# Filling TensorE's wait before the end of every leaf with products that nobody reads

## What is computed

```python
def _L0_attn_ref(x, Wq, bq, Wk, bk, Wv, bv, Wo, bo):
    ...
    def step(carry, qkv):
        A, M = carry
        q, k, v = qkv
        s_t = jnp.sum(k * q, axis=-1, keepdims=True)
        u = k / (jnp.linalg.norm(k, axis=-1, keepdims=True) + EPS)
        Au = jnp.einsum('bij,bj->bi', A, u)
        denom = 1.0 + jnp.sum(u * Au, axis=-1, keepdims=True)
        A = A - jnp.einsum('bi,bj->bij', Au, Au) / denom[..., None]
        z = Au / denom
        alpha = s_t * z
        M = M + jnp.einsum('bi,bj->bij', v, alpha)
        o = jnp.einsum('bij,bj->bi', M, q)
        return ((A, M), o)
...
x = x + 0.5 * _L0_ffn_ref(_layernorm(x, axis=-1), L0_ffn_W1, L0_ffn_b1, L0_ffn_W2, L0_ffn_b2)
x = x + _L0_attn_ref(_layernorm(x, axis=-1), L0_attn_Wq, L0_attn_bq, L0_attn_Wk, L0_attn_bk, L0_attn_Wv, L0_attn_bv, L0_attn_Wo, L0_attn_bo)
x = x + 0.5 * _L0_ffn_ref(_layernorm(x, axis=-1), L0_ffn_W1, L0_ffn_b1, L0_ffn_W2, L0_ffn_b2)
```

## Time and profile before

| | us |
|---|---|
| median of 3 timed runs | 1063.75 |
| lowest and highest | 1062.14, 1065.49 |
| profiled execution | 1061.38 |
| its span, first to last instruction | 1059.7 |

### The profile page before, as it was taken

The page is one execution under the profiler, slowest core; times in us unless marked ns, Lnnn a source line. Parts: engine busy times, 40 slices in busy tenths (PEclk is TensorE's granted clock), DMA queues, the critical chain, the costliest instruction groups (busy, mean ns, idle before and its releaser), DMA issues.

```text
span 1059.7 us, 28459 instructions
## 1 busy us (share of the span) xinstructions
PE 921.2 (87%) x11675; PEld 710.7 (67%) x11675; DVE 786.7 (74%) x2504; ACT 544.5 (51%) x1096; POOL 304.7 (29%) x256
## 2 busy tenths in 40 slices
PE   4899999999998687588898838747799999999998
PEld 1477777777786666476796636546577777777766
DVE  6878788878679998887597979792666665665663
ACT  5678788878745344122344311101565665565574
POOL 4354445444311000000000000003756455455340
PEclk9899999999999898689899859786999999999999
DMA  5353639465437462144500000465524334234231
GB/s 161 70 140 87 166 98 213 127 138 131 121 119 213 146 158 61 41 123 120 161 21 2 5 4 4 135 135 135 130 61 114 86 92 116 73 101 100 40 80 60
DMA packets 170886, 108.28 MB, mean 102 GB/s; under 512 B 79360, under 2 KB 163712, under 8 KB 170112
## 3 DMA queue, kind: packets, MB, share of 16 engines
q1 hardware_dynamic: 153856, 89.62, 33.5%
q10 hardware_dynamic: 16896, 16.78, 5.2%
HBM read 44.96 MB, written 37.75 MB: 78 GB/s over the span
## 4 chain that ended last, share of the span: by engine, by line
PE 31%; DVE 15%; issue 2%; POOL 1%; DMA 1%; ACT 0%; SPq 0%; DVEq 0%; POOLq 0%
PE ldl_work L2043 10%; PE ldl_work L2031 10%; DVE lane_rows L1171 6%; DVE ldl_rank_one L1168 4%; PE ldl_work L2015 2%; DVE ldl_lane_dinv L1153 2%; PE ldl_work L1625 1%; PE ldl_work L2006 1%; PE ldl_work L1999 1%; PE ldl_work L1998 1%; DVE lane_rows L1149 1%; PE ldl_work L1985 1%; DVE lane_rows L1147 1%; PE ldl_work L1360 1%; PE ldl_work L1443 1%
## 5 line engine op out<-in xcount | busy, mean ns | idle before, releaser
L1796 POOL TENSOR_TENSOR T<-T,out_bv_rows 128x512 f32<-128x512 f32 x16 | 20.3, 1271 | 399.4 <-DVE out_s_over_d L1899 393.1
L446 DVE TENSOR_TENSOR ffn_h_rest<-ffn_ps_h,ffn_h_high 128x512 f16<-128x512 f32 x128 | 86.3, 685 | 53.7 <-ACT ffn_ps_h L631 53.2
L630 ACT ACTIVATE ffn_h_high<-ffn_ps_h,b_columns 128x512 f16<-128x512 f32 x128 | 87.9, 686 | 62.5 <-PE ffn_ps_h L712 62.0
L2043 PE MATMUL ldl_work<-w_ternary,ldl_panels 128*128 128x256 f16 x512 | 118.2, 273 | 0.0
L726 PE MATMUL ffn_ps_y<-w_ternary,ffn_h_high 128*128 128x256 f16 x512 | 117.8, 273 | 0.0
L726 PE MATMUL ffn_ps_y<-w_ternary,ffn_h_rest 128*128 128x256 f16 x512 | 117.8, 273 | 0.0
L712 PE MATMUL ffn_ps_h<-ffn_xT_high,w_ternary 128*128 128x512 f16 x256 | 98.6, 385 | 8.5 <-DVE ffn_h_rest L446 8.3
L712 PE MATMUL ffn_ps_h<-ffn_xT_rest,w_ternary 128*128 128x512 f16 x256 | 98.5, 385 | 0.0
L2031 PE MATMUL ldl_work<-out_xT_high,w_ternary 128*128 128x512 f16 x256 | 97.0, 379 | 0.0
L2031 PE MATMUL ldl_work<-out_xT_rest,w_ternary 128*128 128x512 f16 x256 | 97.0, 379 | 0.0
L1944 ACT ACTIVATE ldl_work<-ldl_work,b_columns 128x512 f32<-128x512 f32 x128 | 84.2, 658 | 0.0
(11 more groups left out here) (214 smaller groups left out, 2287.5 us busy)
## 6 DMA issues: line engine op xcount, KB each, us to landing
ffn_x<-in_x SPq DMA_DIRECT2D x16, 512.0 KB, 4.4
x_scratch<-ffn_x_out ACTq DMA_DIRECT2D x16, 512.0 KB, 3.3
aT_scratch<-ffn_aT SPq DMA_DIRECT2D x16, 512.0 KB, 5.1
inv_aT<-aT_scratch SPq DMA_DIRECT2D x16, 512.0 KB, 5.1
T<-x_scratch SPq DMA_DIRECT2D x16, 512.0 KB, 3.8
uT_scratch<-ffn_uT SPq DMA_DIRECT2D x16, 256.0 KB, 5.2
inv_uT<-uT_scratch SPq DMA_DIRECT2D x16, 256.0 KB, 4.1
qT_scratch<-inv_qT SPq DMA_DIRECT2D x16, 256.0 KB, 4.1
```

Of the source, the lines that this page charges most:

```text
L446: nc.vector.tensor_tensor(hl[n % 2][:, f], ps_h[f % 3][:], hh[n % 2][:, f], ALU.subtract).then_inc(hl_done, 1)
L630: nc.scalar.activation(hh[n % 2][:, f], ps_h[f % 3][:], ACT.Gelu, bias=c.b1[:, f:f + 1])
L2043: ins = nc.tensor.matmul(ps_y[t % 2], part[k % 2][:, f, t * P:(t + 1) * P], c.w2[:, f], start=(f == 0 and part is hh), stop=(f == FC - 1 a ...
```

## The change

`stay_busy` is new: it makes `count` products of the 128x128 identity with itself repeated four times (128x512, f32) into a bank of PSUM that nobody reads before it is written anew. `before_leaf_ends(r)` puts such products in front of each wait for `turned`: 7, 5, 5 and 3 in the first factorisation, into the new bank `ps_idle`; 2, 17, 5 and 15 in the second, into the first bank of the area that is filled next, after the wait for that area. Three more stand behind `turn_dots` at the end of the first program, and three in `turn_z(0)` behind the waits for what is emptied and in front of the wait for the rows. The jump of L1433, one line that runs three times in each factorisation, is removed.

```diff
--- before.py
+++ after.py
@@ -843,6 +843,12 @@
                 yield 4 * ((phase + q) % 4) + t, q
 
 
+def stay_busy(nc, c, bank, count):
+
+    for _ in range(count):
+        nc.tensor.matmul(bank, c.ident[:], c.ident[:].unsqueeze(1).to_broadcast([P, GROUP, P]), start=True, stop=True)
+
+
 def bank_order():
     for phase in range(4):
         for q in range(4):
@@ -914,6 +920,7 @@
         ps_v = psum("ps_v", [P, HC, H])
 
         ps_dots = psum("ps_dots", [P, GROUP, P])
+        ps_idle = psum("ps_idle", [P, GROUP, P])
         dots_rows = sb("dots_rows", [NP, P])
 
     diag_done = sem("diagonal_done")
@@ -1348,6 +1355,16 @@
                 next_block(r)
 
     def tensor(pe):
+        def before_leaf_ends(r):
+
+            count = ((7, 5, 5, 3) if first else (2, 17, 5, 15))[r - 1]
+            if first:
+                stay_busy(nc, c, ps_idle[:], count)
+            elif count:
+                what = fills_of(r)[0]
+                free(pe, r, what)
+                stay_busy(nc, c, area(r, what)[:, 0:GROUP], count)
+
         def done(r, what):
 
             free(pe, r, what)
@@ -1428,9 +1445,7 @@
             k = r - 1
             work = area(r, "diagonal")
             emptied_of(pe, k, "panel")
-
-
-            pe.addr_align(256, offset=128, max_nops=0)
+            before_leaf_ends(r)
             pe.wait_ge(turned, r)
             for p, q in tile_order():
                 i = nc.tensor.matmul(work[rows_of(q), p, W:2 * W], T_of[rows_of(q), :, p],
@@ -1502,6 +1517,7 @@
             e.products.tensor_rest(pe)
         for r in range(1 if first else 0, NW + 1):
             if r == NW:
+                before_leaf_ends(NW)
                 pe.wait_ge(turned, NW)
             if first and 0 < r < NW:
                 dots(r - 1)
@@ -1519,6 +1535,7 @@
             if first and r == NW:
                 dots(r - 1)
                 turn_dots()
+                stay_busy(nc, c, ps_idle[:], 3)
             if r < NW - 1:
                 finish_diagonal(r + 1)
 
@@ -1973,6 +1990,7 @@
                 pe.wait_ge(e.stored, e.all_stored)
                 pe.wait_ge(e.emptied, e.all_emptied)
                 pe.wait_ge(e.half_emptied, 1)
+                stay_busy(nc, c, ps_s, 3)
             if n % 4 == 0:
                 pe.wait_ge(e.rows_in[n // 4], 16)
             for k in range(GROUP):
```

## The result

| | before | after |
|---|---|---|
| median of 12 runs each, one chip | 1064.75 | 1069.78 |
| lowest and highest | 1062.14, 1066.4 | 1064.09, 1074.6 |
| profiled execution | 1061.38 | 1066.27 |
| its span | 1059.7 | 1064.5 |
| mean granted clock | 0.929 | 0.958 |

Ratio 1.0049 with a 95% interval of 1.0033 to 1.0064: the change makes the kernel 0.49% slower, where 0.57% faster was forecast. The clock did rise, and the time rose with it.

A forecast was written before the change was run, and what follows sets the result against it. PE's products after each leaf's end bound the path, partly at half clock. Gains of 2.9 + 1.4 (last ends), 1.4 (inner ends) and 0.4 (barrier) sum to 6.1 us: 1057.6 from 1063.75, 0.57% faster, range 1054.5 to 1064.5.

The forecast's parts named there:

- The filler at the end of a long idle time: Last leaf ends: 0.9 us per product, covered by the leaf; L1360 stays at full clock, gaining 2.9 + 1.4 = 4.3 us.
- The barrier: End of the first factorisation: three fillers just covered; first L1625 behind it faster, bounds 0 and 0.6, taken 0.4 us.
- They start earlier by that much: After the last leaf: store and load of W and load of x stay next late, and start earlier by the gain.
- Inner ends, 1.4 us: Six inner leaf ends: 2.85 us if the clock holds through L1436 to L1443, half of it taken.
- The jumps: Behind inner leaf ends: removal moves fetch boundaries to where the instruction count puts them; the jumps themselves cost nothing now.
- Bounds: full gain, or the present end: Inner ends without the jumps: each gets the whole clock gain or ends as now, depending on the stall's place.
- All fit: Fillers before leaf ends, 1.8 to 15.3 us, fit the idle times of before and leave 1.1 to 1.9 us.
- My places of the boundaries: Fetch boundaries estimated some 30, 130, 130, 85, 10 and 240 records into L1436, off by ten or so.
- Rival C: Slower by overrun: fillers begun at half clock run past leaf ends, 2.9 us each; 5.5 us slower, 1069.3; chance 0.07.
- Rival A: The gap moves: faster work lengthens idle time before the next end, the clock falls again; 2 us, 1061.7; chance 0.22.
- D: Identity on identity, nearly all zeros, might not keep the clock; only jumps are left, within 1 us, 1063.7; chance 0.08.
- The two rules that were weighed: Fetching hidden behind dispatch: jumps' removal nil, inner ends 3.9 us; weight load without clock term: sum 1.4 us less.

The follow-up runs named there:

- early loads: Kernel before, jumps kept, fifteen fillers at the last leaf end, three before the rows, loads of bv, bo, wo issued earlier: 1061.35 against 1064.97, ratio 0.9971.
- one jump back: Changed kernel with one of six jumps restored, before the second end of the second factorisation: 1062.32 against 1065.16 for before, ratio 0.998.
- bridge: One filler product added between L1451 and L1458, with inner fillers, on before: 1062.9 (jumps to 224, early loads), 1064.47 (jumps to 128), against 1065.25.
- the narrow fillers: Changed kernel, five fillers before the third end of the second factorisation one column wide instead of 512: 1067.81 against 1064.21 for before, ratio 1.0024.

## Why the prediction was wrong

**The filler at the end of a long idle time: right, at one of the two ends by luck.** 0.9 us each, clock held, L1377 at 3.72 twice: -1.4 and -2.9 as in the sum. The -1.4 was not safe: the same three fillers lost the clock in two other kernels. The barrier gave 1.0 us where 0.4 was taken: the fillers were covered (504.78 to 507.62, PE released at 508.45), the first L1642 took 1.16 for 1.67, and the DMA that it waits for came 0.5 sooner.

**"They start earlier by that much": wrong.** The step took the chain of before, store of the rows and load of x, to move as a whole. It did not ask what stands in front of them in SyncE's queue once the slow L1360 no longer covers it. Four loads there, issued 2 us ahead of the rows in before, now lie directly in front of them. The load of x went at +15.73 for +15.05 and the tail is 0.3 us longer instead of 2.9 shorter; with early loads x goes at +12.73, and the tail is 0.8 shorter than in before.

**Inner ends, 1.4 us: wrong, nearly 0.** The mid value lay between bounds of 0 and 2.85, with no row for a half-busy stretch at full clock. The chip chose the lower bound: L1451's 2.04 us, the same at either clock, and 1.07 us idle behind it were enough for the grant to go at five of six, and it went at the sixth soon after. That isn't so in every run: with one jump back it held without a bridge through the first end of the first factorisation and all but the last 0.2 us of the third. L1436 did stay at 2.02 to 2.04. Where the clock was held the gain was 0.4 to 0.55 us (1.5 to 1.65 for 2.08), less than the 0.7 taken from the 1.32 of L1420.

**The jumps: the step that turned the sign.** "Bounds: full gain, or the present end" looked at the boundaries inside the 256 records behind each leaf end. There it was even right in kind: after has no stall of more than 0.22 us in L1451 and L1458. But the jump also sets where the stalls fall in the whole leaf that follows, and with "All fit" I set the fillers against the idle times of before. Between the second and third ends of the second factorisation before has stalls of 1.34, 2.33 and 1.89 us, after has

```profile
629.92 1.98 PE L1377 MATMUL ldl_work<-ldl_panel,ldl_T_turned 32*32 32x32 f32 x123 [1.31 <-issue]
...
633.81 5.70 PE L1377 MATMUL ldl_work<-ldl_right_side,ldl_T_turned 32*32 32x128 f32 x127 [1.72 <-issue]
...
642.37 1.47 PE L1397 MATMUL ldl_work<-ldl_panels 32*32 32x32 f32 x128 [0.76 <-issue]
...
645.83 0.68 PE L1397 MATMUL ldl_work<-ldl_panels 32*32 32x32 f32 x31 [1.99 <-issue]
```

and then the 1.33 and 1.60 shown at the top: 8.7 us for 5.6. With 1.4 us more for an L1384 at half clock (6.19 us for 4.80) PE comes to the fillers 44.8 us after the second end's products began, where before was done with L1420 after 39.8. These 5.0 us, 4.5 of them in the rows named, take the 6.1 us of idle time down to 1.0. Nothing in the working bounded the arrival. My places of the boundaries were fair where they can be checked, at the three ends of the second factorisation: stalls stand 168, 258 and 244 records on from the start of L1451, where I had 85, 10 and 240 and a block is some 128 records (213 and 266 one and two blocks on), so two lie within the ten and one is 45 off. They were an answer to the wrong question.

**Rival C named the mechanism** (fillers begun at half clock that run over the leaf's end), at this very end, and gave it 0.07. Its price for one such end, 2.9 us, took PE to arrive as in before, 6.1 us early; 1.0 us early it cost 5.36 at the products, 4.7 at the end. Its 6.3 us for two slow products and three fast was right (6.42, the clock back at about 672), and would have just about fitted; what it lacked was a term for the arrival, and it was said to decide where fillers don't bring the clock back, which they did. **Rival A** was right for the inner ends, by another road: the idle time ahead of the leaf's end had not grown (2.03 us at most, and besides the late end none at two inner ends of the first factorisation, where the products began 0.25 and 0.06 us after the leaf's end, the second no later than without fillers); the grant went in the light stretch behind it. **D** fell: the identity on itself kept and brought back the clock.

**The two rules that were weighed.** The Trainium skill (Runtime: NRT & Kernel Launch, section Instruction fetch mechanics) has fetching hidden behind dispatch. By its rule the removal of the jumps was nil; taking them out alone cost 6.6 us here, with stalls of 1.99 and 2.06 us at one leaf end, so the rule doesn't hold for these streams of short products. The Trainium skill (TensorE: Matmul & The Clock Gate, section LDWEIGHTS) gives the load no term of the clock: L1436 agrees, 2.04 us at both, L1461, products and loads together, does not, 1.65 for 2.08.

**What stays open.** The twelve runs of after spread over 10 us, and the profiled one lies 3.5 below the median; where the others lose isn't seen, and the narrow fillers leave the median 3.6 above before although its profile is as fast as before's. One candidate is in the profiles, though no run tests it: the idle time that the fillers are counted against is itself not fixed. Before the third end of the first factorisation it is 6.11 us in before and 3.50 in its repeat, of one and the same program, and five fillers need 4.5. Whether the stretch ahead of the first leaf, 2.6 us longer in after, is noise is open too: over all profiles it runs from 312.35 to 316.1. So the third end of the second factorisation is shown as the main loss of the profile, and by the single jump as worth more than the whole difference in the medians; the sizes between agree only to some 2 us.

## What to carry to other kernels

Filler work is sized by the slack *after* the change, and by the smallest of several profiles: work out when the engine gets there with every other edit in place, and what the fillers cost if the clock is at half when it does. A jump or a few instructions more set where all later instruction stalls fall, up to the next jump; so look at the whole stretch behind it and not at the products next to it. When a slow step on the path gets faster, list what other work its length was hiding, above all in the queues of DMA issues.

## What the runs showed of the hardware

- PE's instructions come in blocks of 256 with two at hand: jumped to the start of a block, it stood for 1.53 to 2.01 us ahead of the 513th instruction, at all six places; 128 records of 32x32 with their loads use up a block in 1.3 to 2.1 us.
- Jumps, with no other edit, moved the median by some 7 us: 6.6 between six jumps and none without fillers, 7.3 by the ratios between one and none with them.
- The clock fell 1.4 us *into* products that followed 2.06 us of idle time, and not at all behind 3.17 us in another kernel: the gap alone does not tell it.
- The same program reached the same wait 6.11 and 3.50 us before its release in two profiles.
- The four stores of the last rows took 7.9 to 9.7 us from first issue to the last landing with four loads issued directly ahead of them, 7.3 to 7.9 with one, and 6.9 to 7.0 where the loads lay 2 us ahead or came behind.
